# Two graph-attention layers on one core: draining the attention sums from PSUM on ScalarE and seeding the next sum there, in a straight list of stages

## What is computed

```python
h = relu(layernorm(x));  x = x + elu(gat(h, W0, a0))      # layer 0
h = relu(layernorm(x));  x = x + gat(h, W1, a1)           # layer 1
# gat(h): Wh = h @ W; e = leaky(e1[i] + e2[j], 0.2); e = where(adj > 0, e, -huge)
#         out = softmax(e, axis=j) @ Wh
```

## Time and profile before

| | us |
|---|---|
| median of 3 runs | 321.0 (320.87 to 323.83) |
| the profiled execution | 320.96 |
| its span, first to last instruction | 319.0 |
| TensorE busy in it | 297.2 |
| VectorE busy in it | 270.1 |
| ScalarE busy in it | 165.4 |

### The profile page before, as it was taken

The page is one execution under the profiler, slowest core; times in us unless marked ns, Lnnn a source line. Parts: engine busy times, 40 slices in busy tenths (PEclk is TensorE's granted clock), DMA queues, the critical chain, the costliest instruction groups (busy, mean ns, idle before and its releaser), DMA issues.

```text
span 319.0 us, 7008 instructions
## 1 busy us (share of the span) xinstructions
PE 297.2 (93%) x2567; PEld 294.8 (92%) x2567; DVE 270.1 (85%) x617; ACT 165.4 (52%) x484; POOL 42.8 (13%) x40
## 2 busy tenths in 40 slices
PE   6889984999999999999999999999999994999695
PEld 6789974999999999999999999999999994999695
DVE  5568479889999989999999989998999679586865
ACT  1586172459394737483684639392757472451300
POOL 3220004300303030303002030303030004000000
PEclk9799998899999999999999999999999998999799
DMA  7991987103576255903593337515480402003011
GB/s 212 396 400 27 310 339 268 64 3 132 156 254 254 77 167 165 386 4 132 198 332 128 132 137 249 207 52 177 149 350 3 134 0 68 0 2 126 8 66 66
DMA packets 15239, 50.45 MB, mean 158 GB/s; under 512 B 2040, under 2 KB 3056, under 8 KB 15216
## 3 DMA queue, kind: packets, MB, share of 16 engines
q1 hardware_dynamic: 15216, 50.14, 43.8%
HBM read 45.88 MB, written 4.26 MB: 157 GB/s over the span
## 4 chain that ended last, share of the span: by engine, by line
PE 75%; DVE 11%; DMA 7%; ACT 3%; issue 1%; SPq 1%; DVEq 0%; ACTq 0%
PE acc L743 57%; PE prj L697 8%; DVE pbuf L527 5%; DMA row_r<-r_rows 4%; PE tp L689 4%; PE acc L761 2%; ACT hp L398 2%; DMA w_ext<-in_w 1%; DMA r_rows<-rT 1%; DVE accs L544 1%; PE prj L700 1%; DVE stats L469 1%; PE acc L727 1%; DVE x L562 1%; DVE x L572 1%
## 5 line engine op out<-in xcount | busy, mean ns | idle before, releaser
L743 PE MATMUL acc<-wh,pbuf 128*128 128x129 f32 x1984 | 235.6, 279 | 10.9 <-DVE pbuf L527 8.2
L743 PEld LDWEIGHTS acc<-wh,pbuf 128*128 128x128 f32 x1984 | 231.4, 195 | 11.7 <-DVE pbuf L527 8.5
L527 DVE SCALAR_TENSOR_TENSOR pbuf<-row_r,sqr,adj_sb 128x1024 f32<-128x1024 f32 x127 | 157.3, 1279 | 12.8 <-DMA row_r<-r_rows 11.8
L398 ACT ACTIVATE hp<-accs,rec 128x128 f32<-128x128 f32 x120 | 36.9, 391 | 65.8 <-DVE rec L554 65.8
L323 POOL TENSOR_TENSOR rstd<-vareps,neg_half 128x8 f32<-128x8 f32 x16 | 33.2, 2074 | 225.8 <-DVE vareps L489 221.9
L359 ACT ACTIVATE xn<-x,shift,rstd 128x128 f32<-128x128 f32 (+1 forms) x123 | 49.0, 483 | 0.0
L380 ACT ACTIVATE wh<-prj,wh 128x128 f32<-128x128 f32 x128 | 34.0, 359 | 0.0
L366 ACT ACTIVATE hT<-tp 128x1024 f32<-128x1024 f32 x16 | 16.4, 1025 | 33.8 <-PE tp L689 33.7
L697 PE MATMUL prj<-w_ext,hT 128*128 128x130 f32 x256 | 31.3, 275 | 0.4 <-ACT hT L366 0.4
L697 PEld LDWEIGHTS prj<-w_ext,hT 128*128 128x128 f32 x256 | 29.9, 191 | 0.6 <-issue 0.6
L469 DVE BATCH_NORM_STATS2 stats<-x 128x6 f32<-128x128 f32 (+1 forms) x128 | 26.3, 280 | 4.5 <-issue 4.4
(11 more groups left out here) (50 smaller groups left out, 133.9 us busy)
## 6 DMA issues: line engine op xcount, KB each, us to landing
adj_sb<-in_adj SPq DMA_DIRECT2D x64, 512.0 KB, 6.1
row_r<-r_rows SPq DMA_DIRECT2D x15, 512.0 KB, 4.3
x<-in_x SPq DMA_DIRECT2D x7, 512.0 KB, 5.6
out_x<-x SPq DMA_DIRECT2D x7, 512.0 KB, 2.9
x<-in_x SPq DMA_DIRECT2D x2, 256.0 KB, 2.9
out_x<-x SPq DMA_DIRECT2D x2, 192.0 KB, 1.9
r_rows<-rT SPq DMA_DIRECT2D x15, 4.0 KB
w_ext<-in_w SPq DMA_DIRECT2D x2, 64.0 KB, 3.9
```

What stands on the lines that cost most here:

```text
L398: op = nc.scalar.activation(hp[:, t, :], accs[:, t, 0:D], ACT.Copy, scale=rec[:, t:t + 1])
L527: nc.vector.scalar_tensor_tensor(pbuf[:, t, :], row_r[:, g, :], sqr[:, g, 0, t:t + 1], adj_at(b, t), ALU.max, ALU.min).then_inc(p_ready, 1)
L743: mm = nc.tensor.matmul(acc[:, k, s * C:(s + 1) * C], pbuf[:, t, i * P:(i + 1) * P], wh[:, g, t, :], start=(t == 0 and s == 0), stop=(t == ...
```

## The change

The stages and their order are the same. What differs:

- **Loops.** The list is written out in Python (`stages`), with no hardware loop. `LATE` = (3, 15).
- **Draining.** `copy_acc` and `scale_accs` are gone, but for stage 0. VectorE only takes the reciprocal of the denominators, bank by bank, out of PSUM (`invert`). ScalarE's `drain` reads each group from PSUM, scales it and writes it to SBUF, and when a bank is drained, `seed` copies the row `uniform` into it, as the base of the next sum. The first matmuls of stage n wait for `acc_seeded` and add to it.
- **Late stages.** In stages 1 and 13 VectorE does the statistics of n+2 after mask 6 (before: after mask 2). ScalarE's `normalise(n+2)` becomes the last work of the stage, and `transposes(n+2)` moves into the next stage, behind attention tile 0; there `project(n+1)` follows tile 2.
- **Residual.** One buffer of six slots for x (`x_sb`) in place of two of three; x stays and is added to.
- **Stage 0.** ScalarE's queue issues half of the first loads. The relu is taken of x minus mean, and 1/std is applied later (`rstd0`, `q_rstd`); hT is copied in two halves; `transposes(1)` comes after attention tile 1, `project(1)` after tile 2, fewer keep-warm transposes.
- **SyncE.** `load_row(n+1)` no longer waits behind the store of a graph.

```diff
 # ScalarE
-            def scale_accs(e):
-                act.wait_ge(rec_ready, e + 1)
-                for t in range(T):
-                    op = nc.scalar.activation(hp[:, t, :], accs[:, t, 0:D], ACT.Copy,
-                                              scale=rec[:, t:t + 1])
+            def seed(n, k):
+                w = tiles_in[k]
+                nc.scalar.activation(acc[:, k, 0:w * C].rearrange("p (s c) -> p s c", c=C),
+                                     uniform[:, n % 2, :].unsqueeze(1).to_broadcast([P, w, C]),
+                                     ACT.Copy).then_inc(acc_seeded, 1)
+            def drain(e):
+                act.wait_ge(hp_free, e)
+                for t, (k, s) in enumerate(bank_of):
+                    if s == 0:
+                        act.wait_ge(rec_ready, 1 + NB * (e - 1) + k + 1)
+                    op = nc.scalar.activation(hp[:, t, :], acc[:, k, s * C:s * C + D], ACT.Copy,
+                                              scale=rec[:, t:t + 1])
...
+                    if k > 0 and s == 0:
+                        act.wait_ge(acc_drained, NB * e + k)
+                        seed(e + 1, k - 1)
+                act.wait_ge(acc_drained, NB * e + NB)
+                seed(e + 1, NB - 1)
 # VectorE
-                nc.vector.tensor_tensor(
-                    accs[:, k * NB:k * NB + w, :],
-                    acc[:, k, 0:w * C].rearrange("p (s c) -> p s c", c=C),
-                    uniform[:, g, :].unsqueeze(1).to_broadcast([P, w, C]),
-                    ALU.add).then_inc(acc_copied, 1)
+            def invert(e, k):
+                dve.wait_ge(acc_done, NB * e + k + 1)
+                den = acc[:, k, 0:w * C].rearrange("p (s c) -> p s c", c=C)[:, :, D]
+                nc.vector.reciprocal(rec[:, k * NB:k * NB + w], den).then_inc(rec_ready, 1)
 # TensorE, attend
-                        pe.wait_ge(acc_copied, NB * (n - 1) + k + 1)
+                            pe.wait_ge(acc_seeded, NB * (n - 1) + k + 1)
```

More of the change, by code:

```diff
@@ L184, in adj_at @@
[L184 to L210, removed]
@@ L299, in _ @@
[L299 to L305, removed]
+                sp.wait_ge(hp_free, stage_of[1, b] + 1)
+                sp.dma_start(ov[b], x_at(b)).then_inc(out_stored[b], 16)
+            sp.dma_start(x_sb[:, 0:HALF * D], xv[0][:, 0:HALF * D]).then_inc(x_half, 16)
+            sp.dma_start(w_tr[:, 0, :], w0t).then_inc(w_in, 16)
@@ new lines, in _ @@
+            load_x(AHEAD + 2)
+            load_row(AHEAD)
+            for n in range(AHEAD, LAST):
+                l, b = stages[n]
+                loads = l == 1 and b + AHEAD < B
+                l_old, b_old = stages[n - 3]
+                if l_old == 1 and b_old + X_SLOTS < B:
+                    load_x(b_old + X_SLOTS)
+                if loads:
+                    for t in range(3):
+                        load_adj(b + AHEAD, t)
+                load_row(n + 1)
+                if loads:
+                    for t in range(3, T):
+                        load_adj(b + AHEAD, t)
+                if stages[n - 1][0] == 1:
+                    store(stages[n - 1][1])
@@ L356, in normalise @@
                 nc.scalar.activation(act_gate[:, :], shift[:, 0:1], ACT.Copy)
[L357 to L358 removed]
+                src = x3_at(stages[m][1])
+                for t in range(T):
                     nc.scalar.activation(xn[:, t, :], src[:, t, :], ACT.Identity,
@@ new lines, in _ @@
+            normalise(1)
+            scale_wh_first(range(3, T - 1))
+            copy_hT(1)
+            scale_wh_first(range(T - 1, T))
+            for n in range(LAST + 1):
+                elu = n > 0 and stages[n - 1][0] == 0
+                if n == 1:
+                    drain_first()
+                elif n > 1:
+                    drain(n - 1)
+                if n + 1 in LATE:
+                    copy_hT(n + 1)
+                    elu_exp(n - 1) if elu else None
+                    normalise(n + 2) if n + 2 <= LAST else None
+                    exps(n + 1)
+                    copy_r(n + 1)
+                elif n + 2 in LATE:
+                    elu_exp(n - 1)
+                    exps(n + 1)
+                    copy_r(n + 1)
+                elif n < LAST:
+                    exps(n + 1)
+                    copy_r(n + 1)
+                    elu_exp(n - 1) if elu else None
+                    normalise(n + 2) if n + 2 <= LAST else None
+                if n < LAST:
+                    scale_wh(n + 1)
+                if n + 2 in LATE:
+                    normalise(n + 2)
+                elif n + 2 <= LAST:
@@ new lines, in _ @@
+            masks(0, (6, 7))
+            for n in range(1, LAST):
+                l, b = stages[n - 1]
+                if n + 2 <= LAST and n + 2 not in LATE and n + 1 not in LATE:
+                    statistics(n + 2)
+                    moments(n + 2)
+                masks(n, (0, 1))
+                take_acc(n - 1)
+                if n + 1 in LATE:
+                    masks(n, (2, 3))
+                    if n + 2 <= LAST:
+                        statistics(n + 2)
+                        moments(n + 2)
+                    copy_e(n + 1)
+                    masks(n, (4,))
+                    exp_args(n + 1)
+                    masks(n, (5,))
+                else:
+                    copy_e(n + 1)
+                    masks(n, (2,))
+                    exp_args(n + 1)
+                    masks(n, (3,))
+                    if n + 2 in LATE:
+                        add_elu(b)
+                        masks(n, (4,))
+                        add_x(b)
+                        masks(n, (5, 6))
+                        statistics(n + 2)
+                        moments(n + 2)
+                        masks(n, (7,))
+                        continue
+                    masks(n, (4, 5))
+                if l == 0:
+                    add_elu(b)
+                    masks(n, (6,))
+                    add_x(b)
+                    masks(n, (7,))
+                else:
+                    add_hp(b)
+                    masks(n, (6, 7))
@@ L674, in _, with keep_warm, turn @@
+            masks(LAST, (0, 1))
+            take_acc(LAST - 1)
+            masks(LAST, (2, 3, 4))
+            add_hp(B - 2)
+            masks(LAST, (5, 6, 7))
+            last()
         @block.tensor
         def _(pe):
+            def keep_warm(count):
+                for _ in range(count):
+                    nc.tensor.transpose(acc[:, 0, 0:P], ident[:, :], ident[:, :])
+            def turn(t):
+                return nc.tensor.transpose(tp[:, t * P:(t + 1) * P], xn[:, t, :], ident[:, :])
@@ new lines, in _ @@
+            keep_warm(WARM[0])
+            pe.wait_ge(w_in, 96)
+            for l in range(2):
+                mm = nc.tensor.matmul(prj[:, 0, 2 * l:2 * l + 2], w_tr[:, l, :], a_cols[:, l, :],
+                                      start=(l == 0), stop=True, skip_group_check=True)
+            mm.then_inc(wa_done, 1)
+            keep_warm(WARM[1])
+            transposes_first()
+            project_first()
+            hsum_first(range(HALF))
+            spread_emax(0)
+            hsum_first(range(HALF, T))
@@ L823 @@
+                    attend(n, (2, 3, 4, 5))
+                if n + 2 <= LAST and n + 2 not in LATE:
+                    transposes(n + 2)
+                attend(n, (6, 7))
+            attend(LAST, range(LAST_SPLIT))
+            attend_last()
 def kernel(x, adj, L0_gnn_W, L0_gnn_a, L1_gnn_W, L1_gnn_a):
```

840 lines of the change are left out of this document (432 added, 408 removed).

## The result

The kernel after takes 336.0 us (median of 4 runs, 335.4 to 337.7), the one before 321.2 in the same comparison: 1.046 times as long (95% interval 1.040 to 1.052). Forecast were 339 and "slower".

The account below looks back on a forecast made before the run. TensorE, busy 297.2 of 319.0 us, was taken to bound the kernel through its chain of waits. Terms summed to +18.1; 319.0 + 18.1 + 1.96 outside the span gave 339, range 328 to 349.

Parts of the forecast that it names:

- start: Before stage 0's attention: loads on two queues, fewer warm transposes; attention from about 16.0 instead of 22.1; -6.1 us.
- stage 1: Masks 3 to 6 no longer stand behind the statistics, so 4.08 us idle and its clock loss go; -4.2 us.
- stage 3: VectorE arrives 3.1 us after the stage's start; 3.0 and 0.5 idle, 1.9 for the clock; +5.4 us.
- stage 15: Row arrives late and two masks precede the reciprocals; 5.0 and 0.5 idle, 1.9 for the clock; +2.9 us.
- The new path: Between two sums: VectorE's reciprocal, ScalarE's scalings out of PSUM, then seeds of 0.50 and 0.39 us into PSUM.
- Even stages: Within stages 4 to 12: VectorE takes over 0.5 us late, so each even stage loses 1.0; +5.2 with odd stages.
- Stages 2 and 14: Drain waits behind late `normalise`: 5.7 us idle before tile 0, 1.9 for the clock; +10.0 and +9.4 us.
- Dear seeds: Rival: seeds take double the assumed time, in steady stages and the four long waits; 356 us, 5% chance.
- the clock falls in even stages: Rival: TensorE's clock also drops in the five even steady stages, 1.9 us each; 349 us, 5% chance.
- the start gains nothing: Rival: weights land as before, first attention at 19 to 22; 342 to 345 us, 10% chance.
- cheap path: Rival: seeds cost nothing, GpSimd's power takes 2.07 not 2.61, the clock holds in stage 3; 329 us, 18% chance.
- VectorE is early enough: Rival: VectorE 4 us ahead of the count in late stages, so ScalarE normalises in time; 318 us, 7% chance.

Follow-up runs that it names:

- experiment 7: As experiment 6, with the transposes of stages 2 and 14 behind attention tile 1 instead of tile 0; 309.6 us, 0.965 of before.
- experiment 4: Kernel after, with VectorE's reciprocals of the finished sums moved between mask 0 and mask 1; 324.1 us, 1.013 of before.
- experiment 3: Kernel after without seeds: uniform row left out of the sums of stages 1 to 15, drain kept; 327.0 us, 1.022 of before.
- experiment 2: Kernel after, with ScalarE draining first and then normalising in stages 2 and 14; 335.2 us, 1.047 of before.
- experiment 6: Kernel of experiment 1, with VectorE's copies of the sums taken between masks 0 and 1; 311.9 us, 0.971 of before.
- experiment 8: As experiment 7, with ScalarE's exponentials and row copy of n+1 ahead of elu's exponential in stages 1 and 13; 312.9 us, 0.976 of before.
- experiment 1: Kernel after with drain and seed undone, VectorE copying the sums out again; 315.8 us, 0.986 of before.
- experiment 5: Kernel after, seed kept, experiments 2 and 4 together, and in stages 2 and 14 transposes behind tile 2, projection behind tile 3; 318.4 us, 0.990 of before.

## Why the prediction was right, and where its sizes were off

| Term | predicted | measured |
|---|---|---|
| start | -6.1 | -5.2 |
| stage 0 | +2.3 | +2.2 |
| stage 1 | -4.2 | -3.2 |
| stage 2 | +10.0 | +9.6 |
| stage 3 | +5.4 | +3.3 |
| stages 4 to 12 | +5.2 | +5.6 |
| stage 13 | -6.4 | -6.5 |
| stage 14 | +9.4 | +8.8 |
| stage 15 | +2.9 | +2.7 |
| tail | -0.4 | -0.4 |
| sum | +18.1 | +16.9 |

- **The bound.** TensorE, by its order and its waits: it stayed so. Freeing VectorE could not help by itself, and experiment 7, with VectorE fuller and TensorE nearly without waits, says the same from the other side.
- **The new path.** Seeds forecast at 0.50 and 0.39 took 0.51, 0.54 and 0.39. The line drawn through two copies out of PSUM fits. The Trainium skill ("ScalarE: Activation LUTs", section "Step-by-step: what each stage is for") says that ScalarE writes to PSUM faster than to SBUF. Nothing here bears that out, and nothing refutes it: the seeds read SBUF and write PSUM, those copies do the reverse, so the two differ in their source as well. The bound "seeds cost nothing" was right in one sense only: in experiment 4 they do cost nothing in steady stages, because they start earlier.
- **Even stages.** 1.0 was forecast, 1.11 measured (five of them, and odd ones at exactly 17.40). Experiments 3 and 4 confirm the cause twice over: no seed, or the same seed one mask (1.24) earlier, and the loss is gone.
- **Stages 2 and 14.** Idle 5.7 forecast, 5.25 both times, with `normalise` just ahead of the drain, as said. Experiment 2 refines the cause: `normalise` holds 2.8 to 3.1 of the 5.25, and the rest is VectorE's two masks and the path behind them. It also shows that the prediction priced the wait and not its removal, which is worth far less.
- **The clock.** Four stretches at half clock were forecast and four came, but not the same: stages 2, 3, 14 and 15 were named, and it was 1, 2, 14 and 15. That the number agrees is luck. The price of 1.9 is also a little high: it sets a busy time of 9.05, which reaches to the end of the last pass, against 7.15 from start to start. At full clock 64 passes show as 7.31 (L761 in before), so that the half clock cost 1.7 in each place of before.
- **Stage 3, the mis-sized term (+5.4, got +3.3).** The idle time was 2.56 and 0.19, not 3.0 and 0.5; and "the clock 1.9, since 3.0 is above the 2.71 that brought it down" did not happen. The windows of after (TensorE's clock is the third number from the end):

```profile
90.00:92.00 2.00, 1.81 (x14) 1.62 (x15) 0.00 (x0) 1.63 (x6) 0.00 (x0) 1.00 0.87 274
92.00:94.00 2.00, 2.00 (x20) 2.00 (x20) 1.39 (x6) 0.44 (x2) 0.00 (x0) 1.00 0.46 178
```

- **Stage 1 (-4.2, got -3.2).** The masks behind the statistics were the right gain, and no tile of this stage waits 4.08 any more. But the first tile waits 2.39 where I had 1.5, and the clock fell there, which I had not counted, and tile 7 waited 0.69 for its mask; the wait at the turn that I had at 2.2 was not there.
- **Stage 15 (+2.9, got +2.7).** The path was as said: the row comes late, two masks follow it, then the reciprocals. Two errors in it cancel. The idle time was 4.10, not 5.0, because the drain began 2.4 after T15 (311.2), not 3.35; the 64 passes behind it took 10.27, 2.96 more than at full clock, where 0.5 and 1.9 had been set.
- **Start.** The weights' matmul came at 8.16 after 1.18 idle, where I had 6.7 (row below). In the kernels of experiments 6 and 8, whose start is the same, it came at 7.06 and 7.20. This may be part of why the profiled execution is 1.7 above its median; no other execution of after has a trace.

```profile
8.16 0.61 PE L856 MATMUL prj<-a_cols,w_tr 128*128 128x2 f32 x4 [1.18 <-DMA w_ext<-in_w]
```

- **The rivals.** "Dear seeds", "the clock falls in even stages" and "the start gains nothing" did not come; the "cheap path" came in one of its three parts, the clock in stage 3. "VectorE is early enough" did not hold, so its price of about 20 us was not tested. Experiments 1 and 5 bring about as much, but by other terms: they give back the 5.6 of the even stages too, which were not in that price.

Not isolated: how much of the 5 us that experiment 1 gains over before is the start, and how much the move of the statistics in stages 1 and 13. The traces give -5.2 for the start, and -6.5 for stage 13 against losses in 14, but no run changed one alone.

## What to carry to other kernels

Before work is moved off a busy engine, ask what the other engine has in its queue at the moment when the result is wanted: 20 us of VectorE's work went away here, and ScalarE's place in the path cost as much. A base written into PSUM by another engine stands in the gap between two sums, an addition on the way out does not. Try the place in the queue first: one mask moved was worth 12 us with the seed and 4 without, and when one wait is removed, look for the next one a tile later. When the queues are in order, look at what feeds them: the waits that experiment 7 leaves follow the row from HBM.

## What was not expected of the hardware

The length of an idle time does not by itself say whether TensorE's clock falls behind it. It fell to 0.50 after 2.39 (stage 1, after), 2.55 (experiment 5, stage 2), 2.56 (experiment 2, stage 3) and 2.71, and held at 1.00 after 2.56 (after, stage 3, windows above) and 2.87. One kernel, that of experiment 1, shows both, falling after the shorter of its two idle times: 1.96 in stage 2, then 2.87 in stage 15.

```profile
59.00:61.00 2.00, 2.00 (x11) 2.00 (x11) 2.00 (x4) 2.00 (x8) 0.00 (x0) 0.50 0.00 0
...
297.00:299.00 2.00, 2.00 (x20) 2.00 (x20) 2.00 (x3) 1.77 (x7) 0.00 (x0) 1.00 0.00 0
```

Of its four executions one kept a mean clock of 1.000 and took 313.8; the other three had 0.989, 0.989 and 0.995 and took 315.5 to 316.1. What decides it was not tried. It is not the whole spread between executions either: in the kernel of experiment 7 the quickest of six (308.8) had 0.992, and two with 1.000 took 310.8.
